# Two-layer graph kernel on one core: the opening of the first two groups in another order, x of group 0 loaded in halves

## What is computed

```python
h = relu(layernorm(x))                       # layer 0: attention
q, k, v = h @ Wq.T, h @ Wk.T, h @ Wv.T
rel = adj.T * (q @ k.T)                      # per graph
x = x + (rel / norm(rel, axis=2)) @ v
h = relu(layernorm(x))                       # layer 1: three gated steps
for _ in range(3):
    a = concat(adj @ h, adj @ h)
    z = sigmoid(a @ w3.T + b3 + h @ u3.T + bu3)
    r = sigmoid(a @ w4.T + b4 + h @ u3.T + bu3)
    c = tanh(a @ w5.T + b5 + (r * h) @ u5.T + bu5)
    h = (1 - z) * h + z * c
x = x + h
```

## Time and profile before

| | |
|---|---|
| Time, median of 3 runs | 953.89 us (952.88 to 955.03) |
| Time of the profiled execution | 949.41 us |
| Its span, first to last instruction | 947.3 us |
| Mean granted TensorE clock | 0.995 |
| PE (TensorE matmul) busy | 913.2 us, 96% |
| DVE (VectorE) busy | 741.1 us, 78% |
| ACT (ScalarE) busy | 518.0 us, 55% |
| POOL (GpSimd) busy | 113.7 us, 12% |

### The profile page before, as it was taken

How to read it: one execution, slowest core, us unless ns; L and a number is a source line. 1 busy time by engine, 2 the same in 40 slices (tenths; PEclk the granted TensorE clock), 3 DMA queues, 4 the chain that set the end, 5 groups by cost and what they waited for, 6 DMA issues and landing times.

```text
span 947.3 us, 14699 instructions
## 1 busy us (share of the span) xinstructions
PE 913.2 (96%) x4816; PEld 777.4 (82%) x4816; DVE 741.1 (78%) x1484; ACT 518.0 (55%) x893; POOL 113.7 (12%) x161
## 2 busy tenths in 40 slices
PE   7789999999999999999999999999999999999997
PEld 6678888888888878788788887888888888888885
DVE  4777778977788886888779877798877987787765
ACT  4446555556546554565536656456555556545552
POOL 1110101301021010210102101120101301011000
PEclk9999999999999999999999999999999999999998
DMA  5014222532235122441324413144231532233112
GB/s 173 2 44 134 88 92 75 175 105 89 89 111 179 65 100 99 135 153 47 131 88 134 168 48 127 55 157 153 75 102 68 169 117 89 89 107 115 68 67 89
DMA packets 75383, 98.73 MB, mean 104 GB/s; under 512 B 8165, under 2 KB 65765, under 8 KB 75365
## 3 DMA queue, kind: packets, MB, share of 16 engines
q1 hardware_dynamic: 75360, 98.50, 31.2%
HBM read 50.76 MB, written 47.71 MB: 104 GB/s over the span
## 4 chain that ended last, share of the span: by engine, by line
PE 62%; DVE 17%; issue 9%; ACT 8%; POOL 3%; DMA 0%; DVEq 0%; POOLq 0%; ACTq 0%; SPq 0%
PE gate L378 9%; PE gate L379 9%; PE gate L380 9%; PE cand L378 6%; PE cand L380 6%; PE cand L379 6%; PE fea L491 5%; DVE c_s L989 3%; PE fea L439 3%; DVE h L833 2%; DVE a_lo L833 2%; POOL rnorm L328 2%; PE tok L378 2%; PE tok L380 2%; PE tok L379 2%
## 5 line engine op out<-in xcount | busy, mean ns | idle before, releaser
L721 ACT ACTIVATE r_s<-gate,b_r 128x512 f32<-128x512 f32 x96 | 65.8, 690 | 160.1 <-PE gate L380 160.1
L984 DVE SCALAR_TENSOR_TENSOR d_s<-z_s,h 128x512 f32<-128x512 f32 x96 | 64.3, 689 | 50.2 <-ACT z_s L734 50.2
L734 ACT ACTIVATE z_s<-gate,b_z 128x512 f32<-128x512 f32 x96 | 63.0, 681 | 43.2 <-PE gate L380 42.7
L378 PE MATMUL cand<-rh_hi,W_hi_u 128*128 128x512 f32 x192 | 77.4, 403 | 8.8 <-DVE rh_lo L833 8.8
L1012 DVE TENSOR_TENSOR rh<-r_s,h 128x512 f32<-128x512 f32 x96 | 63.5, 689 | 27.4 <-ACT r_s L721 27.4
L378 PE MATMUL gate<-a_hi,W_hi_w 128*128 128x512 f32 x192 | 77.0, 401 | 5.5 <-DVE a_lo L833 5.5
L642 ACT ACTIVATE h_hi<-h 128x512 fp32r<-128x512 f32 x92 | 57.3, 630 | 44.1 <-DVE h L833 26.7
L989 DVE TENSOR_TENSOR c_s<-z_s,c_s 128x512 f32<-128x512 f32 x96 | 64.3, 670 | 21.3 <-ACT c_s L740 21.3
L642 ACT ACTIVATE rh_hi<-rh 128x512 fp32r<-128x512 f32 x96 | 58.2, 629 | 36.3 <-DVE rh L1012 34.6
L378 PE MATMUL gate<-h_hi,W_hi_u 128*128 128x512 f32 x192 | 77.8, 405 | 0.0
L380 PE MATMUL cand<-rh_hi,W_lo_u 128*128 128x512 f32 x192 | 75.1, 391 | 0.0
(11 more groups left out here) (128 smaller groups left out, 2251.6 us busy)
## 6 DMA issues: line engine op xcount, KB each, us to landing
h_back<-h_trip SPq DMA_DIRECT2D x244, 128.0 KB, 2.8
h_trip<-h_turned SPq DMA_DIRECT2D x47, 512.0 KB, 2.7
x_s<-x SPq DMA_DIRECT2D x16, 512.0 KB, 4.6
out<-o_s SPq DMA_DIRECT2D x16, 512.0 KB, 3.0
hx_trip<-hx SPq DMA_DIRECT2D x14, 512.0 KB, 3.4
hx_back<-hx_trip SPq DMA_DIRECT2D x56, 128.0 KB, 2.8
h_trip<-h_blk SPq DMA_DIRECT2D x14, 512.0 KB, 3.0
z_s<-w_t SPq DMA_DIRECT2D x1, 512.0 KB, 4.1
```

Source lines behind the costliest of these rows:

```text
L378: nc.tensor.matmul(dst, l_hi, r_hi, start=start, stop=False, skip_group_check=True)
L721: nc.scalar.activation(r_s[:, c, :], gate[:, c, :], ACT.Sigmoid, bias=b_r[:, c:c + 1]).then_inc(r_ready, 1)
L734: nc.scalar.activation(z_s[:, c, :], gate[:, c, :], ACT.Sigmoid, bias=b_z[:, c:c + 1]).then_inc(z_ready, 1)
L984: nc.vector.scalar_tensor_tensor(d_s[:, c, :], z_s[:, c, :], 1.0, h[s][:, c, :], ALU.subtract, ALU.mult).then_inc(diff_ready, 1)
```

## The change

One group's chain stands ahead of the other's in all lists; values of group 0 are made in halves; the transposes of group 1 and the first ones of h0 go to `cand` instead of `tok`, by quarters, with semaphores of their own (`turned_full`, `turned_taken`); TensorE starts queries before `hxT_lo` is there; `W_hi_m` is made by DVE instead of ACT; the u3 products of step 0 stand ahead of the weighted sum of group 1; step 0 has candidate_a ahead of update_gate, as in the loop; norms of group 1 go through `cand`, and are taken ahead of the split of S; loads have semaphores of their own and another order. In the loop itself only counters and names differ. The diff, cut to its core (helpers that only take another source or semaphore are left out):

```diff
-    TOK_START = ["split x 0", "v 0", "split x 1", "sum 0", "v 1", "new first", "sum 1", "new 0"]
+    TOK_START = ["split x 0", "v 0", "sum 0", "v 1", "sum 1", "new 0"]
-    FEA_START = ["q 0", "rel 0", "norm 0", "q 1", "rel 1", "adj first", "norm 1", "adj 0"]
+    FEA_START = ["q 0", "rel 0", "norm 0", "q 1", "rel 1", "adj first", "adj 0"]
...
 # SP
-            load_x(0, 0)
+            sp.sem_inc(x_in[0], 16)
+            for b in range(2):
+                part = slice(HQ * b, HQ * b + HQ)
+                sp.dma_start(x_s[0][:, part, :], x_g[0][:, part, :]).then_inc(x_first[b], 16)
...
+            load_x(1, 1)
             sp.dma_start(raw["v"].rearrange("p (c n) -> p c n", c=C),
...
-            load_x(1, 1)
+            load_w("w4", w4_t)
+            load_u("u3", u3_t)
             sp.wait_ge(const_zero, 1)
...
+                for q in range(Q):
+                    sp.dma_start(mask[part, q, part], adj).then_inc(mask_in, 16)
+            load_w("w5", w5_t)
+            load_w("w3", w3_t)
...
                 sp.dma_start(adjT[part, part], adj_t).then_inc(adj_in, 16)
...
+            load_u("u5", u5_t)
...
 # POOL
             inverse_std(0, 0)
+            pool.wait_ge(hx_ready, Q)
             inverse_std(0, 1)
             inverse_norm(fea_taken, 2 * n("norm 0") + 2)
             inverse_std(1, 0)
-            inverse_norm(fea_taken, 2 * n("norm 1") + 2)
+            inverse_norm(norm_taken, 1)
...
 # TensorE
+            def queries_start(g, n, lo_ready):
+                for o in range(C):
+                    fea_wait(n, o)
+                    for c in range(C):
+                        pe.wait_ge(hxT_hi_ready, 2 * g + (c + 1))
+                        nc.tensor.matmul(fea[:, o, :], weight("m", c, o)[0], hxT_hi[:, c, :], start=c == 0, stop=False,
+                                         skip_group_check=True)
+                    for c in range(C):
+                        nc.tensor.matmul(fea[:, o, :], weight("m", c, o)[1], hxT_hi[:, c, :], start=False, stop=False,
+                                         skip_group_check=True)
+                    for c in range(C):
+                        pe.wait_ge(lo_ready, c + 1)
+                        last = nc.tensor.matmul(fea[:, o, :], weight("m", c, o)[0], hxT_lo[:, c, :], start=False,
...
-            pe.wait_ge(attn_w_in, 48)
+            pe.wait_ge(qk_in, 32)
...
-            transpose_hx(0, n("split x 0"))
+            transpose_hx(0, tokT, tok_full)
             pe.wait_ge(w_lo_ready, 1)
-            queries(0, n("q 0"), n("split x 0"))
+            queries_start(0, n("q 0"), tok_taken)
             pe.wait_ge(w_lo_ready, 2)
-            values(0, n("v 0"))
+            pe.wait_ge(hxT_copied, 2)
+            values(0, n("v 0"), (0,))
             scores(n("rel 0"), n("q 0"))
-            transpose_hx(1, n("split x 1"))
+            values(0, n("v 0"), (1,))
             norms_start(0, n("norm 0"))
-            weighted_sum(0, n("sum 0"), n("v 0"))
-            queries(1, n("q 1"), n("split x 1"))
+            transpose_hx(1, cand, turned_full)
+            weighted_sum_start(0, n("sum 0"))
+            queries_start(1, n("q 1"), turned_taken)
             values(1, n("v 1"))
+            pe.wait_ge(hxT_copied, 4)
             scores(n("rel 1"), n("q 1"))
-            pe.wait_ge(h0_ready, Q)
-            transpose_new(0, 0, n("new first"))
+            transpose_new(0, 0, cand, turned_full)
+            pe.wait_ge(adj_in, 32)
             adjacency(0, h0[0], n("adj first"))
             adjacency(1, h0[0], n("adj first"))
+            reset_gate_h_start()
+            norms(1, 0)
+            weighted_sum_start(1, n("sum 1"))
             pe.wait_ge(w_lo_ready, 4)
-
-            norms_start(1, n("norm 1"))
-            weighted_sum(1, n("sum 1"), n("v 1"))
-            tok_done(n("new first"))
-            reset_gate(0, 0, n("adj first"))
+            reset_gate_a(0, 0, n("adj first"))
+            candidate_a(0, 0, 1)
             update_gate(0, 0)
-            candidate_a(0, 0)
-            pe.wait_ge(h0_ready, 2 * Q)
-            transpose_new(1, 1, n("new 0"))
+            tok_done(n("sum 1"))
+            transpose_new(1, 1, tokT, tok_full)
+            candidate_rh(0, 0)
             adjacency(0, h0[1], n("adj 0"))
-            candidate_rh(0, 0)
             adjacency(1, h0[1], n("adj 0"))
...
 # ACT
             normalise(0, 0, 0)
-            act.wait_ge(m_full, 1)
-            split_weight(0, "m", gate[:, 0, :])
-            split_hx_start(n("split x 0"))
-            act.wait_ge(attn_w_in, 48)
-            split_weight(0, "v", raw["v"])
+            split_hx_start(tokT, tok_full, tok_taken)
+            split_weight(v_w_in, 16, "v", raw["v"])
             normalise(0, 1, 1)
-            split_v(n("v 0"))
-            split_S(n("rel 0"))
-            split_hx_start(n("split x 1"))
-            act.wait_ge(gate_w_in, 16 * 5)
-            split_weight(0, "u3", raw["u3"])
-            split_weight(1, "w4", sum4)
+            split_v(n("v 0"), (0,))
+            split_weight(gate_w_in["u3"], 16, "u3", raw["u3"])
+            split_weight(w_sum, 1, "w4", sum4)
+            square_S(n("rel 0"))
+            round_S(n("rel 0"))
+            split_v(n("v 0"), (1,))
+            split_hx_start(cand, turned_full, turned_taken)
+            split_weight(w_sum, 2, "w5", sum5)
+            split_v(n("v 1"), (0,))
             normalise(1, 0, 0)
-            split_v(n("v 1"))
-            split_new_start(0, n("new first"))
-            split_S(n("rel 1"))
+            split_new_start(0, cand, turned_full, 2)
+            split_v(n("v 1"), (1,))
+            square_S(n("rel 1"))
             split_a(0, 0, n("adj first"))
             split_a(0, 1, n("adj first"))
-            split_weight(2, "wz", sumz)
+            round_S(n("rel 1"))
+            split_weight(w_sum, 3, "wz", sumz)
+            split_weight(gate_w_in["u5"], 16, "u5", raw["u5"])
...
             normalise(1, 1, 1)
+            split_new_start(1, tokT, tok_full, 2 * n("new 0"))
             update_sigmoid(0)
-            split_new_start(1, n("new 0"))
+            candidate_tanh(0)
             split_a(1, 0, n("adj 0"))
             split_a(1, 1, n("adj 0"))
-            candidate_tanh(0)
...
 # DVE
-            statistics(0, 0, 0, 1)
+            for b in range(2):
+                dve.wait_ge(x_first[b], 16)
+                stats_part(0, 0, range(HQ * b, HQ * b + HQ))
+            stats_end(0, 0)
             shifts(0, 0)
+            dve.wait_ge(x_in[1], 16)
+            stats_part(0, 1, range(HQ))
             dve.wait_ge(m_full, 1)
-            split_weight(1, "m", gate[:, 0, :])
-            split_hx_start(0, n("split x 0"))
-            split_weight(2, "v", raw["v"])
-            statistics(0, 1, 1, 1)
+            nc.vector.tensor_copy(W_hi["m"][:].rearrange("p c n -> p (c n)"), gate[:, 0, :]).then_inc(m_hi_ready, 1)
+            dve.wait_ge(m_hi_ready, 1)
+            sub(W_lo["m"][:].rearrange("p c n -> p (c n)"), gate[:, 0, :],
...
+            stats_part(0, 1, range(HQ, Q))
+            split_hx_start(0, tokT, tok_full, tok_taken)
+            stats_end(0, 1)
+            take_q(n("q 0"), (0,))
+            split_weight(1, "v", raw["v"])
             shifts(0, 1)
-            take_q(n("q 0"))
-            split_v(0, n("v 0"))
-            dve.wait_ge(adj_in, 16 * 2 * (1 + Q))
+            take_q(n("q 0"), (1,))
+            dve.wait_ge(gate_w_in["w4"], 16)
+            nc.vector.tensor_tensor(sum4, raw["w4"][:, 0, :], raw["w4"][:, 1, :], ALU.add).then_inc(w_sum, 1)
+            split_v(0, n("v 0"), (0,))
+            split_weight(2, "u3", raw["u3"])
+            dve.wait_ge(mask_in, 16 * 2 * Q)
             mask_scores(n("rel 0"))
+            split_weight(3, "w4", sum4)
+            take_norm_start(n("norm 0"))
             split_S(0)
-            split_hx_start(1, n("split x 1"))
-            take_norm_start(n("norm 0"))
...
+            split_v(0, n("v 0"), (1,))
+            split_hx_start(1, cand, turned_full, turned_taken)
+            dve.wait_ge(gate_w_in["w5"], 16)
+            nc.vector.tensor_tensor(sum5, raw["w5"][:, 0, :], raw["w5"][:, 1, :], ALU.add).then_inc(w_sum, 1)
             add_attention(0, 0, n("sum 0"))
             statistics(1, 0, 0, n("sum 0"))
-            split_weight(3, "u3", raw["u3"])
+            take_q(n("q 1"))
             shifts(1, 0)
-            take_q(n("q 1"))
-            split_weight(4, "w4", sum4)
+            split_v(1, n("v 1"), (0,))
...
             mask_scores(n("rel 1"))
-            take_new_start(0, 0, n("new first"))
-            split_S(1)
+            take_new_start(0, 0, cand, turned_full, 2, turned_taken)
+            split_v(1, n("v 1"), (1,))
             split_a(0, 0, 0)
             split_a(0, 0, 1)
...
+            take_norm(1)
+            split_S(1)
+            split_weight(4, "w5", sum5)
             dve.wait_ge(bias_in, 16 * 5)
...
             split_weight(5, "wz", sumz)
-
-            take_norm_start(n("norm 1"))
```

(43 more changed lines are left out.)

147 lines of the change are left out of this document (80 added, 67 removed).

## The result

The changed kernel takes 940.00 us, the median of 4 runs (939.46 to 942.36), against 953.38 (950.19 to 955.03) of the kernel before beside it: a ratio of 0.987, 95% interval 0.985 to 0.990. On the second occasion, in the experiments, it was 941.87 against 952.66, 0.989 (0.987 to 0.991). It is 13.4 and 10.8 us faster, where 8.7 were forecast; 940.0 and 941.9 lie outside the range (942.8 to 949.5). The profiled execution took 939.46, span 937.6, mean clock 0.998. One execution of the kernel before, in the experiments, took 4306.73 us at a clock of 1.00; it is in no ratio and no table here, and its cause isn't known.

A forecast was written before the change was run, and what follows sets the result against it. TensorE was taken as the bound, with 13.4 us idle in the opening; 4.2, 3.1 and 1.4 us won there make 8.7, taking the median from 953.89 to 945.2 us, with an 8-in-10 range of 942.8 to 949.5.

The forecast's parts named there:

- The new clock of the opening: Timetable of the changed opening up to the loop, putting the first c_s at 55.3 instead of 64.02 us.
- The three parts of the sum: Opening: 4.2 us to group 1's weighted sum, 3.1 to the end of the transposes, 1.4 to c_s; 8.7 together.
- (A): Rival: thin TensorE stretches at 19.7 to 22.5 and 35.5 to 40.1 lower the clock; gain 3 to 7 us; chance 0.22.
- (D): Rival: low clock from the first weighted sum into the loop makes the kernel slower, 968 us; chance 0.04.
- the signs of being wrong: First c_s later than 59, low clock after 40, DMA releasing DVE in the opening, or a round not 113.93 us.
- Halves worth 0: Loading x of group 0 in halves was booked at 0 us, as hxT_lo waits for DVE until 11.5.
- lands earlier: Load of x of group 1: with v now behind it, it lands earlier than the present 8.9 us.
- The loss of some tenths: Loading x in halves: by the skill's batching rule a loss of some tenths, leaving the sum the same.
- the 5.9 given as its bound: Load of w4: 4.1 to 5.9 us after issue, so landing at 8 to 10, wanted at 15.5.
- W_hi_m on DVE: Opening, group 0: DVE copies W_hi_m out of PSUM, taken as 0.69 us against ACT's 0.57.
- (B): Rival: DVE's queue runs free, leaving only TensorE's work; gain 10.5 to 13.4 us, about 942; chance 0.06.
- (C): Rival: a late input or missed queue order at the join holds step 0 at the old time, 953.9; chance 0.06.

The follow-up runs named there:

- a_tanh_late: The changed kernel with the tanh of step 0 behind both a_hi copies again, as before the change: 944.01 us (943.12 to 946.86).
- a_again: The changed kernel, unchanged, run a second time: 941.87 us (941.45 to 942.18), ratio 0.989 to the kernel before.
- a_m_act: The changed kernel with W_hi_m made by ACT again instead of DVE: 941.26 us (940.80 to 942.15).
- b_again: The kernel before, unchanged, run against itself: 953.70 us, median of 12 (949.18 to 955.45), ratio 1.000.
- a_whole_x: The changed kernel with x of group 0 loaded whole again instead of in halves: 941.13 us (940.29 to 942.39), ratio 0.988.
- b_fill_all: The kernel before with idle products in six TensorE waits of the opening and the tanh of step 0 ahead of the a_hi copies: 946.99 us against 952.43.
- b_u3_early: The kernel before with the u3 products of step 0 ahead of the second norms and the weighted sum of group 1: 951.51 us, ratio 0.999.
- a_norm_first: The changed kernel with norms of group 1 ahead of the u3 products and DVE's wz split behind adding attention and statistics: 939.71 us, ratio 0.987.
- a_norm_whole: The changed kernel with norms of group 1 ahead of the u3 products, wz split later and x of group 0 loaded whole: 940.17 us, ratio 0.986.

## Why the prediction was wrong

Wrong is the size: 8.7 us forecast, 13.4 and 10.8 measured, for a change that did what the working said.

- **The new clock of the opening** was right. The places compared above, on TensorE, DVE and ACT, from 10.95 to 59.5, lie within 0.4 us of the trace; the largest misses are the second shift and normalise, 29.67 and 29.86 instead of 30.05 and 30.2, since POOL's power took 1.01 us and not 1.38. `c_s` at 55.3 was 55.11. The three parts of the sum, 4.2, 3.1 and 1.4, came out as 4.2 (44.32 to 40.15), 3.3 (13.8 to 10.5) and 1.5 us (5.9 to 4.5), the last confirmed by a_tanh_late (1.5).
- **The failing step** is the sentence "The median of the runs is 953.89, and the same 8.7 us off it give 945.2". The sum was made against an execution that took 949.41, 4.5 us less than the median and below all three runs shown. That gap was noted and not asked about; the term put at nothing is what the clock costs the usual execution of the kernel before beyond the one that was profiled. The profiled execution had one stretch at the low level ahead of `c_s`, 53 of the 67 have a lower mean clock than it, the one of these that was traced has three such stretches and pays 4.0 us for them at `c_s`, and by the table the classes differ by up to 5 us. The change fills what comes ahead of them. In its place: 8.9 us at the loop's door off the 949.8 of the class that the profiled execution was in, which makes 940.9; the two sets measured are at 940.0 and 941.9. Against the median of all 67, 952.99, that is 12 us, 3 of them what the executions of the kernel before differ by, which goes with the clock.
- **The clock in the rivals** stood only on the side of loss, (A) and (D). (A) was right that thin stretches remain and named the place, ahead of 40: a_again falls there and pays 1.6 us for it, against the 1.7 worked out. A low clock after 40 stood among the signs of being wrong, and a_again and a_m_act show it; the first trace of the changed kernel doesn't. The same reasoning, used on the kernel before, would have pointed at the missing 3 us (two more dips at 1.7 are 3.4). The table of stretches had 41.3 to 43.9 empty with the clock still up, and I read that as evidence that such a wait is harmless; b_again has the same wait at 43.5 and the clock falls at 46.5.
- **The sample.** The Trainium skill ("TensorE: Matmul & The Clock Gate", Part 1) says beside the rule that was cited that the gate's count doesn't start with the kernel, so that one kernel meets it differently from run to run. b_again agrees: three dips where the first trace has one, with the same program. With that sentence, the one dip of the first trace should have been read as a sample.
- **Loads.** Halves worth 0: right (a_whole_x). x of group 1 "lands earlier", at about 7: wrong, it still took 5.9 us and DVE waited for it until 8.92, so the order of v behind it bought nothing there (DMA issues of its first 3.4 us: count, KB, us to landing):

```profile
x_s<-x SPq DMA_DIRECT2D x2, 256.0 KB, 2.8
x_s<-x SPq DMA_DIRECT2D x1, 512.0 KB, 5.9
```

It had no effect, since m came at 9.5. The loss of some tenths that was allowed for the halves didn't show either: hx starts 0.8 us earlier with them (7.09 against 7.88 in a_whole_x). w4 took 7.0 us, more than the 5.9 given as its bound, and was still hidden.
- **What m waits for** was overlooked. In the kernel before its products wait for q, k and v (`attn_w_in, 48`), in the changed one for q and k alone. In two traces of kernels built on the one before, b_fill_all and b_u3_early, v came so late that m started at 8.83 and 9.07. TensorE's timeline of b_u3_early:

```profile
9.07 1.99 PE L608 MATMUL gate<-d_s 128*128 128x256 f32 x8 [1.06 <-DMA o_s<-wv_t]
```

No trace of the changed kernel or its variants has that wait. It is worth about 1.1 us at the start of m when it comes; how much of the median it makes wasn't measured.
- **W_hi_m on DVE** at 0.69: 0.69 measured (the CAST row), and its move worth nothing (a_m_act), where the sum hadn't booked anything for it by itself.
- **The other rivals.** (B) is out as it was told: 4.9 us of idle TensorE stay, and DVE's queue isn't free. The measured gains fall into its bracket, 10.5 to 13.4, but that is luck: they come from the schedule of the forecast and from the clock. (C) and (D) didn't come.

## What to carry to other kernels

A sum made against one profiled execution holds for that execution; if the median of the runs is 0.5% away, find out first what differs, and the granted clock of each run is the first column to look at. An idle stretch of TensorE cost twice here, once as idle time and, in a part of the executions, once more behind it as products at 1.2 GHz; so a reordering that fills such stretches can win more than its schedule says. Filling all of them with idle products showed how much, and filling three of them didn't. Where one engine's queue order is changed, work out the whole new timetable: hand-over by hand-over it came within 0.4 us here, while one part tried alone (b_u3_early) ran into the next bound.

## What was not expected of the hardware

The 16 products at the very start (32 records) take 5.26 to 6.74 us, although nothing they need differs, and in twelve of the fourteen traces m starts right behind them, between 7.31 and 8.79. The same products take 0.119 us a record later (b_fill_all, 22 in 2.62 us) and 0.164 to 0.21 there. Counted in half microseconds, they change their rate on the way, and at another time in each execution. The first trace of the kernel before at 5 and at 6 us, and then a_norm_first, by the view of stretches (TensorE's records are in the first brackets):

```profile
5.00:5.50 0.50, 0.50 (x5) 0.50 (x5) 0.50 (x3) 0.00 (x0) 0.00 (x0) 1.00 0.96 301
6.00:6.50 0.50, 0.50 (x7) 0.50 (x6) 0.42 (x7) 0.00 (x0) 0.00 (x0) 1.00 1.08 375
```

```profile
5.00:5.50 0.50, 0.50 (x4) 0.50 (x4) 0.46 (x4) 0.00 (x0) 0.00 (x0) 1.00 0.73 238
6.00:6.50 0.50, 0.50 (x4) 0.50 (x4) 0.00 (x0) 0.00 (x0) 0.48 (x1) 1.00 1.04 322
```

The kernel before goes from 4 or 5 records a slice to 7 at about 5.5 us and a_again at about 7; a_norm_first stays at 4 or 5 to the end of these products at 8.9, which is 0.21 us a record. That is 1.7 times the 0.119 of later, close to the 2.69/1.52 = 1.77 of the weighted sum at the two levels. So the reading is that the first of them run at the low level; the granted clock says 1.00 throughout and doesn't show the level of the very start.

Everything of group 0 stands behind m. In the two traces in which m starts at 8.78 and 8.61 (a_norm_first, a_norm_whole) the first weighted sum is at 23.58 and 23.43, where the changed kernel, with m at 7.60, has 22.50. So up to a microsecond and a half of the difference between two executions can be this start, beside the dips. Fewer of these products weren't tried.
